# A cross-attention and mixture-of-experts kernel: shared gate and up products from float32r parts split by GpSimd, in another order, with some expert weights loaded later

## What is computed

```python
h = _rmsnorm(_layernorm(x), rms_weight)          # 2048 tokens x 512
logits = h @ router_w                            # 8 experts, top 2 kept
g = jnp.einsum('td,edf->tef', h, w_gate)         # experts, F = 256
u = jnp.einsum('td,edf->tef', h, w_up)
eo = jnp.einsum('tef,efd->ted', silu(g) * u, w_down)
moe = jnp.einsum('te,ted->td', w_dense, eo)
sh = (silu(h @ sw_gate) * (h @ sw_up)) @ sw_down # shared expert, 256 wide
out = x + moe + sh
```

## Time and profile before

| | |
|---|---|
| median of 3 runs | 854.7 us (854.08 to 859.1) |
| profiled execution, own time | 855.44 us |
| its span, first to last instruction | 853.7 us |
| mean granted TensorE clock | 0.994 |
| busy share of the span: PE, PEld, DVE, ACT, POOL | 95%, 45%, 61%, 47%, 39% |
| shared gate and up products (L1254) | 128 matmul records |
| expert gate and up products (L1371) | 312 records, 140.4 us |
| expert block to expert block | some 5.5 us |

### The profile page before, as it was taken

One profiled execution on the slowest core, in us unless ns is written; L12 is line 12 of the kernel. 1 busy time (PEld: TensorE's weight loads), 2 busy tenths in 40 slices (PEclk: granted clock), 3 DMA queues, 4 the chain that ended last, 5 costly groups with the idle time before them and its releaser, 6 DMA issues. The chain is left out here.

```text
span 853.7 us, 11389 instructions
## 1 busy us (share of the span) xinstructions
PE 809.5 (95%) x3747; PEld 384.6 (45%) x3747; DVE 517.8 (61%) x1043; ACT 401.2 (47%) x751; POOL 330.9 (39%) x274
## 2 busy tenths in 40 slices
PE   7999999999999999999999998999999999999993
PEld 2434434334344343343433454443545555555552
DVE  5787888787787877877878654568542222222221
ACT  1115666667677677676776663110423223333221
POOL 4207316226154072252100211000117777777774
PEclk9999999999999999999999999999999999999997
DMA  8948556546665567466533223931726565555553
GB/s 270 217 89 224 116 125 165 131 103 143 143 137 125 118 157 134 114 147 152 123 78 105 91 77 106 406 118 50 255 53 100 93 97 95 99 88 97 95 97 43
DMA packets 54956, 110.48 MB, mean 129 GB/s; under 512 B 12580, under 2 KB 27684, under 8 KB 50660
## 3 DMA queue, kind: packets, MB, share of 16 engines
q1 hardware_dynamic: 37852, 80.23, 37.2%
q0 software_dynamic: 16960, 29.37, 18.2%
q10 hardware_dynamic: 88, 0.16, 0.1%
HBM read 68.44 MB, written 41.16 MB: 128 GB/s over the span
## 5 line engine op out<-in xcount | busy, mean ns | idle before, releaser
L926 DVE TENSOR_REDUCE negmax<-front_ps 128x1 f32<-128x512 f32 x512 | 323.4, 681 | 89.3 <-PE front_ps L779 88.9
L688 ACT ACTIVATE probs<-st_ps 128x512 f32<-128x512 f32 x512 | 280.2, 601 | 169.9 <-PE st_ps L813 153.2
L1178 POOL DMA_INDIRECT out<-x_sb,row_i x78 | 122.0, 1564 | 72.1 <-ACT x_sb L1226 59.0
L1371 PE MATMUL big_ps<-w_gu,attn 128*128 x312 | 140.4, 593 | 0.8 <-ACT attn L1218 0.8
L1565 DVE TENSOR_TENSOR zeros<-attn,big_ps 128x256 f32<-128x256 f32 x39 | 16.4, 421 | 116.3 <-ACT attn L1238 116.3
L391 POOL TENSOR_TENSOR attn<-attn,recip 128x512 f32<-128x512 f32 x15 | 19.2, 1277 | 174.9 <-DMA recip<-rec_dram 174.9
L813 PE MATMUL st_ps<-stacks 50*128 50x512 f32 x256 | 77.6, 488 | 5.5 <-ACT probs L688 4.4
L1371 PEld LDWEIGHTS big_ps<-w_gu,attn 128*128 128x128 f32 x312 | 56.2, 190 | 56.9 <-issue 56.9
L813 PE MATMUL st_ps<-q_stack,k_stack 50*128 50x512 f32 x256 | 74.6, 491 | 3.9 <-ACT probs L688 2.8
L779 PE MATMUL front_ps<-stacks 48*128 48x512 f32 x256 | 68.6, 434 | 3.4 <-DVE negmax L926 2.7
L1238 ACT ACTIVATE attn<-big_ps 128x256 f32<-128x256 f32 x39 | 15.0, 384 | 117.7 <-PE big_ps L1371 117.7
(11 more groups left out here) (189 smaller groups left out, 1024.8 us busy)
## 6 DMA issues: line engine op xcount, KB each, us to landing
parts_dram<-early SPq DMA_DIRECT2D x32, 512.0 KB, 6.0
stacks<-parts_dram SPq DMA_DIRECT2D x32, 256.0 KB, 5.6
w_gu<-in_gate_up SPq DMA_DIRECT2D x8, 1024.0 KB, 13.3
x_sb<-in_x SPq DMA_DIRECT2D x8, 512.0 KB, 10.6
early<-in_ctx POOLq DMA_DIRECT2D x8, 512.0 KB, 7.0
stacks<-parts_dram SPq DMA_DIRECT2D x32, 128.0 KB, 6.0
k_stack<-parts_dram SPq DMA_DIRECT2D x16, 256.0 KB, 4.7
q_stack<-parts_dram SPq DMA_DIRECT2D x16, 256.0 KB, 5.8
```

The source lines that it names most:

```text
L688: nc.scalar.activation(probs[:, k % 2, u % GH, :], score_bank(UNITS * s + u), ACT.Exp, scale=SCALE).then_inc(exp_done, 1)
L926: nc.vector.tensor_reduce(negmax[:, n % 2, c:c + 1], smax_bank(UNITS * n + u), AX_X, ALU.max, negate=True).then_inc(max_done, 1)
L1178: nc.gpsimd.indirect_dma_start(outs[i], bass.IndirectOffsetOnAxis(ap=row_i[:, k:k + 1], axis=0), y_sb[:, k % RING, DY * i:DY * (i + 1)], N ...
L1371: mm = nc.tensor.matmul(gu_ps[:, :], h_t[:, k % 2, a, :], w_gu[:, bass.ds(expert, 1), a, :], start=(a == 0), stop=(a == DT - 1))
```

## The change

The shared gate and up products are made from float32r parts, as the attention's projections are. GpSimd makes the parts: of the shared gate and up weights in half 14 (`sh_gu_high` in the place of the attention's projection weights, `sh_gu_low` in the place of the weights themselves), of h in four groups of 512 tokens (`split_ht`), a group's parts being a CAST and a subtraction of 128 x 2048. Groups 0 and 1 stand in half 15 around the division of half 14's numerators, groups 2 and 3 in the second block, each behind the stores of its tiles. A pair is now 24 float32r matmuls instead of 8 float32 ones.

PE takes pair 1 ahead of the tiles turned first and pair 2 ahead of the output products; all later pairs move up by one place.

The parts need room. The masks now lie where the rows of h of groups 0 to 2 were, in an order that lets each be written once PE is through with the pairs of those groups (`shgu_ready`), and expert down weights 0 to 5 (`KEPT = 6`) are loaded after the look-up. The weights `w_gu` of expert 0 lie in the place of `sh_gu_high` and are loaded after pair 7, ahead of down weights 6 and 7.

```diff
+        ht_high = stacks[:, :].rearrange("p (g a t) -> p g a t", a=DT, t=GT * P)
+        ht_low = down_high[:, :].rearrange("p (g a t) -> p g a t", a=DT, t=GT * P)
...
+        w_parts = asb("w_parts", [P, 2 * 3 * CT * C], F32R)
+        w_low, w_high = (w_parts[:, 3 * CT * C * i:3 * CT * C * (i + 1)].rearrange("p (i o c) -> p i o c", i=3, c=C) for i in range(2))
+        sh_gu_high = w_parts[:, 0:DT * 2 * F].rearrange("p (a f) -> p a f", a=DT)
+        sh_gu_low = c_high[:, :, :, :].rearrange("p i o t -> p (i o t)").rearrange("p (a f) -> p a f", a=DT)
...
+        def split_ht(pool, g):
+
+            pool.wait_ge(h_stored, 16 * (2 * GT if g < 2 else GT * (g + 1)))
+            pool.wait_ge(h_turned, GT * (g + 1))
+            pool.wait_ge(lg_ready, GT * (g + 1))
+            nc.gpsimd.tensor_copy(ht_high[:, g, :, :], ht_all[:, g, :, :]).then_inc(ht_high_ready, 1)
+            pool.wait_ge(ht_high_ready, g + 1)
+            nc.gpsimd.tensor_tensor(ht_low[:, g, :, :], ht_all[:, g, :, :], ht_high[:, g, :, :].bitcast(F32),
+                                    ALU.subtract).then_inc(ht_split, 1)
...
+                    if s == HALVES - 2:
+                        pool.wait_ge(shared_loaded, 16 * 2)
+                        nc.gpsimd.tensor_copy(sh_gu_high, sh_gu[:, :, :]).then_inc(sh_high_ready, 1)
+                        pool.wait_ge(sh_high_ready, 1)
+                        nc.gpsimd.tensor_tensor(sh_gu_low, sh_gu[:, :, :], sh_gu_high.bitcast(F32), ALU.subtract).then_inc(sh_split, 1)
                     if s == HALVES - 1:
                         for t in range(STORED):
                             store_h(pool, t)
+                        split_ht(pool, 0)
                     if s > 0:
                         divide(pool, s - 1)
+                    if s == HALVES - 1:
+                        split_ht(pool, 1)
...
-        KEPT = 2
+        GROUP = GT * D
+        KEPT = 6
...
-                for e in range(E):
+                for e in range(1, E):
                     sp.dma_start(w_gu[:, e, :, :], gate_up[e]).then_inc(wgu_loaded, 16)
-                sp.wait_ge(h_stored, 16 * NTILE)
-                sp.wait_ge(h_turned, NTILE)
-                for e in range(KEPT):
-                    sp.dma_start(w_dn[:, e, :, :], down[e]).then_inc(wdn_loaded[e], 16)
...
                 sp.wait_ge(found_ready, 1)
+                for e in range(KEPT):
+                    sp.dma_start(w_dn[:, e, :, :], down[e]).then_inc(wdn_loaded[e], 16)
+                sp.wait_ge(shgu_ready, FT * GROUPS)
+                sp.dma_start(w_gu[:, 0, :, :], gate_up[0]).then_inc(wgu_loaded, 16)
                 for e in range(KEPT, E):
...
-                for t in range(STORED, NTILE):
+                for t in range(STORED, EARLY):
                     store_h(pool, t)
+                split_ht(pool, 2)
+                for t in range(EARLY, NTILE):
+                    store_h(pool, t)
+                split_ht(pool, 3)
...
                     for i in which:
+                        cols = slice(i * F + c * P, i * F + (c + 1) * P)
                         for a in range(DT):
-                            mm = nc.tensor.matmul(big_ps[:, 2 * (j % 2) + i, :], sh_gu[:, a, i * F + c * P:i * F + (c + 1) * P],
-                                                  ht_all[:, g, a, :],
-                                                  start=(a == 0), stop=(a == DT - 1))
+                            for p, (w, h) in enumerate(((sh_gu_high, ht_high), (sh_gu_high, ht_low), (sh_gu_low, ht_high))):
+                                mm = nc.tensor.matmul(big_ps[:, 2 * (j % 2) + i, :], w[:, a, cols], h[:, g, a, :],
+                                                      start=(a == 0 and p == 0), stop=(a == DT - 1 and p == PRODUCTS - 1))
...
                 shared_gates(0)
+                shared_gates(1)
                 turn_h(pe, EARLY)
                 turn_h(pe, EARLY + 1)
-                shared_gates(1)
+                shared_gates(2)
                 out_last(0)
                 out_last(1)
...
-                dve.wait_ge(h_stored, 16 * NTILE)
-                dve.wait_ge(h_turned, NTILE)
+                dve.wait_ge(shgu_ready, 2 * FT)
...
+                dve.wait_ge(shgu_ready, 3 * FT)
```

More of the change, by code:

```diff
@@ L121, in xattn_ffn_kernel @@
         ht_all = early[:, :].rearrange("p (g a t) -> p g a t", a=DT, t=GT * P)
+        ht_high = stacks[:, :].rearrange("p (g a t) -> p g a t", a=DT, t=GT * P)
+        ht_low = down_high[:, :].rearrange("p (g a t) -> p g a t", a=DT, t=GT * P)
+        sh_high_ready = sem("sh_high_ready")
+        sh_split = sem("sh_split")
+        ht_high_ready = sem("ht_high_ready")
+        ht_split = sem("ht_split")
         h_part = sem("h_part")
@@ L151, in stack @@
             return asb(f"{name}{i}", [P, PAIRS, T], F32R)
+        with ExitStack() as same_place:
+            w_t = sb("w_t", [P, 3, CT, C], F32, same_place)
+        w_parts = asb("w_parts", [P, 2 * 3 * CT * C], F32R)
+        w_low, w_high = (w_parts[:, 3 * CT * C * i:3 * CT * C * (i + 1)].rearrange("p (i o c) -> p i o c", i=3, c=C) for i in range(2))
+        sh_gu_high = w_parts[:, 0:DT * 2 * F].rearrange("p (a f) -> p a f", a=DT)
+        sh_gu_low = c_high[:, :, :, :].rearrange("p i o t -> p (i o t)").rearrange("p (a f) -> p a f", a=DT)
         q_stack = [stack("q_stack", i) for i in range(NBUF)]
@@ L165, in xattn_ffn_kernel @@
         nm_parts = asb("nm_parts", [HH * TT, PARTS, P], F32R)
-        with ExitStack() as same_place:
-            w_t = sb("w_t", [P, 3, CT, C], F32, same_place)
-        w_low = asb("w_low", [P, 3, CT, C], F32R)
-        w_high = asb("w_high", [P, 3, CT, C], F32R)
         smax_ps = front_ps
@@ L1204, in _ @@
                 turn_h(EARLY + 3)
+                silu(3)
                 act.wait_ge(gap_ready, 1)
                 nc.scalar.activation(small[:, 3, :], small[:, 2, :], ACT.Exp).then_inc(egap_ready, 1)
-                for j in range(3, FT * GROUPS):
+                for j in range(4, FT * GROUPS):
                     silu(j)
@@ L1248, in shared_gates @@
                     g, c = j // FT, j % FT
-                    pe.wait_ge(ht_ready, GT * (g + 1))
+                    if j == 0:
+                        pe.wait_ge(sh_split, 1)
+                    pe.wait_ge(ht_split, g + 1)
                     if j >= 2:
@@ L1286, in _ @@
                 logits(pe, EARLY + 1)
-                shared_gates(2)
+                shared_gates(3)
                 turn_h(pe, EARLY + 2)
@@ L1295, in _ @@
                 shared_down(3)
-                shared_gates(3, (0,))
+                shared_gates(4, (0,))
                 pe.wait_ge(chosen_ready, 1)
@@ L1302, in _ @@
                                  ).then_inc(cnt_ready, 1)
-                shared_gates(3, (1,))
-                shared_gates(4)
+                shared_gates(4, (1,))
                 shared_gates(5)
```

8 lines of the change are left out of this document (4 added, 4 removed).

## The result

The changed kernel takes 866.9 us (median of 6 runs, 865.1 to 870.1), the kernel before 854.35 in the same comparison: a ratio of 1.015, 95% interval 1.0131 to 1.0168. It is slower by 1.5%. The profiled execution is the longest of the six: 870.1 us of its own time with a span of 868.1, so 14.4 us of span more than before where the medians differ by 12.5.

What follows compares the result with a forecast made beforehand. PE, busy 95% of the span, was taken as the bound, though it waits for DVE in between. Terms -3.8 + 2.8 + 0.9 + 4.0 + 3.3 + 4.7 = +11.9 us gave a median of 866, range 859 to 873.

Steps and rivals of the forecast that it cites:

- last attention step: Splits of groups 0 and 1 hold DVE's tiles 9 and 10, PE waits for tile 10: +4.0 us.
- behind it: Behind the attention part: output products 0.8 us later for three pairs ahead, 3.3 more from group 2's split holding tile 12.
- table, held: Token table: group 3's cast and subtraction hold two chained DVE operations, +4.7 us.
- wait for pair 3: DVE's wait of 1.85 us for pair 3 goes, since PE has it done long before: -1.9 us.
- pairs 6, 7, clock, weights: End of the stretch: pairs 6 and 7 on PE's chain -2.7, slow clock +2.8, later weights +0.9 us.
- The holds: DVE operations reading SBUF, with one or two inputs, wait until GpSimd's whole instruction ends, at three places: +4.0, +3.3, +4.7 us.
- The first rival: Only one-input DVE forms are held, at the attention step and behind it, not in the table: +2.4 us, 857, chance 0.22.
- My clock term: PE's new long wait ahead of 586.8 drops its clock to half speed behind it: +2.8 us, bounds 0 and 3.3.
- further slow clock: PE's waits in the holds may cost more half-speed time; named for the range 859 to 873 only, no size given.
- The faster products: Shared gate and up pairs take 5.5 us instead of 6.87: 11 us over all eight, not all on the chain.
- The weights loaded later: The last down weight lands near 621, delaying the first expert product: +0.9 us, bounds 0 and 3.7.
- second and third rivals: No hold that matters: 854.6, chance 0.20; the same with clock held and weights in time: 851, faster ones 0.10.

Runs made afterwards that it cites:

- filled runs: The changed kernel with six or three products of zeros on TensorE ahead of the turn of tile 10, in its wait: 867.6 and 865.2 us.
- the one with no full split: The changed kernel with GpSimd's splits of h cut to 2 columns for all four groups, shared expert's values wrong: 855.9 us, ratio 1.0012.
- the kernel in pieces: The changed kernel, complete, with each split of h as four casts and four subtractions of 512 columns instead of two instructions of 2048: 858.2 us.
- the kernel in pieces with pair 6 moved: The changed kernel with splits of h in 512-column instructions and gate pair 6 ahead of the down products of tiles 6 and 7: 852.4 us.

## Why the prediction was right

The forecast was 866, the median is 866.9, and the cause was the one named. The terms, from the profiled run against that of before:

| place | predicted | measured | how |
|---|---|---|---|
| last attention step | +4.0 | +7.9 | pair 0 at 529.24, was 521.36 |
| behind it | +0.8 +3.3 | +3.3 | output products at 549.22, was 538.07: +11.2 |
| from there to the table | 0 | +1.7 | 571.89, was 559.05: +12.8 |
| table, held | +4.7 | +4.6 | second pick at 580.27, was 562.86: +17.4 |
| wait for pair 3 | -1.9 | -2.0 | down products at 603.31, was 587.90: +15.4 |
| pairs 6, 7, clock, weights | +1.0 | +0.2 | first expert product at 638.68: +15.6 |
| expert part | 0 | -1.2 | span +14.4 |

- **The holds.** The step "a DVE operation in this form is held until GpSimd's instruction is through, and I take the whole for two SBUF inputs" was right, and it decided. The trace of before had the one-input form alone (0.91 us); now L1470 and L1471, with two, are held too. The first rival, one-input forms only, falls by them. The order of who comes first at a gap was right: first half behind the cast, second half behind the subtraction.
- **The last attention step** is the term that was mis-sized. I had +4.0 for PE's wait with scores and exponentials behind it. The hold was taken too long: the second cast ran at 509.22 and not near 512, tile 10 was ready at 516.31 and not at 517.7, and the wait was 2.58. What was missing is the clock: 4.4 us of it up to the last tile's logits, as the filled runs show, and 0.8 on these logits (1.85 us, 1.03 before). My clock term stood at the long wait alone; I named "further slow clock" for the range and didn't price it.
- **The clock behind the long wait.** 6.49 us instead of 3.67: +2.8, as taken. The Trainium skill (TensorE: Matmul & The Clock Gate, "What's actually happening") says that activity lifts the level; by this the filled wait should keep it, and the run agrees: 1.00 in three windows where the change has 0.68, 0.50 and 0.50.
- **Behind it and in the table** 3.3 for 4.1 and 4.6 for 4.7. That the first is right in size owes something to luck: I had PE waiting there for tiles 12 and 13. It didn't wait at all, since the two pairs took 13.5 us at a partly slow clock and covered the hold.
- **From there to the table** I had nothing, and 1.7 us were lost: the down products of tiles 0 and 1 took 5.29 us instead of 3.60, at a clock of 0.70. No hold lies there. With the same waits ahead of these products (1.2 and 0.5 us) both filled runs and the one with no full split have them at 3.60, while the kernel in pieces has 5.29. Why the clock falls there in some profiles only stays open.
- **The faster products**: 5.56 us a pair, as 24 times 0.23 has it, and DVE's wait for pair 3 is gone. The kernel with no full split measures everything but the holds at once: -3.8 + 2.8 + 0.9 = -0.1 was worked out, the ratio is 1.0012, +1.0 us with an interval of -0.4 to +2.6.
- **The weights loaded later** cost nothing that can be seen in the change, 0.9 taken, since PE itself had fallen back to where they land. Where PE is early they end last: in the kernel in pieces with pair 6 moved, the chain runs through that load for 12.8 us, and the first expert product starts 1.78 us after the block's turn begins instead of 1.37, 0.4 late.
- **The sum** of the terms, +11.9, met the medians' +12.5 partly by luck. Against the profiled run (+14.4) the last attention step is 3.9 short and the stretch to the table 1.7. The other terms and the expert part are some 3 too high in sum and take more than half of that back, and the profiled run has 1.9 more than the medians.

The second and third rivals (no hold) are what was measured with the splits cut: 855.9, not 854.6 or 851. They were right about the rest of the change and wrong about the hold.

## What to carry to other kernels

An idle GpSimd is not free for VectorE: before work of 128x2048 is put there, look which VectorE operations lie beside it, and keep scalings and sums that read only SBUF away (reductions and statistics of the same tiles ran free), or cut GpSimd's work into short instructions; that alone took back 8.7 of the 12.5 us here. A wait of 2.6 us on TensorE can cost 4.4 more behind it, so price a new wait with its clock, and put ready work into it: moving one gate pair gained 3.7 to 8.6 us, in the old kernel too. When an engine gets faster, ask first whether it was the one waited for: over eight pairs 10.5 us of products were saved, and without the holds the time stayed the same until the order was changed.

## What the runs showed of the hardware that I had not expected

- The hold seems to work both ways. A subtraction of 128x2048 that began with a longer VectorE operation in its gap took 4.83 to 4.94 us, 4.58 in the table, where the operation in the gap was one of 0.29 us, and 4.56 for the shared weights, where only reductions and statistics lay at its start.
- What is held and what is not, beside GpSimd work: held were a tensor_scalar of 128x512 with one SBUF input (0.49 to 4.65 us), a scalar_tensor_tensor with two (0.74 to 1.83) and a tensor_tensor of 128x128 with two (0.29 to 4.63). Not held were reductions (0.29), statistics (0.69) and additions with one input in PSUM (0.69). The Trainium skill (SBUF — State Buffer, "SBUF: two separate sides") has the lock for two-port modes and for two SBUF inputs; before, only a row with one SBUF input was there; the runs now show holds with one and with two.
- A slow clock can be a cover: with the clock kept up behind the first wait, PE waited 2.42 us ahead of tile 12, where the change has no wait.
- Short waits can be followed by half clock too, and not each time. Behind the same wait of 0.97 or 0.98 us ahead of the last tile's logits the granted clock from 520 to 525 us is 1.00 in the kernel before and 0.66 in the one with no full split. So what a wait costs in clock is read from the profile of each kernel, and one profile needn't stand for all runs.
